# A reordered setup, the first tokens on SyncE's queue, and fill products in the projection's last step

## The reference, cut to what matters

```python
xn = layernorm(x)
# mixer
proj = xn @ in_proj_w + in_proj_b; v = proj[..., :d]
for i in range(2):
    ctrl = proj[..., (i + 1) * d:(i + 2) * d]
    h = implicit_filter(...)        # sin/cos of time -> gelu -> gelu -> linear, times exp(-|decay| t L)
    v = fft_conv(v, h)              # causal convolution over 2048
    xc = depthwise_conv3(ctrl) + conv_b
    v = v * xc * sigmoid(xc @ gate_w + gate_b)
attn = v @ out_proj_w + out_proj_b
# feed-forward: tern(w) = clip(round(w / scale), -1, 1), scale = mean |w| by row
r = relu(xn @ (tern(w_fc) * s).T + gate * (xn @ v.T @ fast_b.T @ u.T))
out = x + attn + (r * r) @ (tern(w_proj) * s).T
```

## Time and profile before

| | us |
|---|---|
| median of three runs | 929.61 (923.80, 929.61, 930.54) |
| profiled execution | 922.28 |
| its span, first to last instruction | 920.4 |
| setup, to the projection's first instruction | 0 to 67.6 |
| projection, to the last engine's block end | 67.6 to 367.2 |
| mixing and the output | 367.2 to 920.4 |

### The profile page before, as it was taken

How to read it: one execution, slowest core, us unless ns; L and a number is a source line. 1 busy time by engine, 2 the same in 40 slices (tenths; PEclk the granted TensorE clock), 3 DMA queues, 4 the chain that set the end, 5 groups by cost and what they waited for, 6 DMA issues and landing times.

```text
span 920.4 us, 25865 instructions
## 1 busy us (share of the span) xinstructions
PE 838.2 (91%) x9894; PEld 699.6 (76%) x9895; DVE 632.2 (69%) x1041; ACT 467.5 (51%) x678; POOL 242.6 (26%) x259
## 2 busy tenths in 40 slices
PE   3837999999999994899999999999999999999995
PEld 1325888888888883678888888788877888788995
DVE  6963799899899885455556555665655556666884
ACT  6422777777777874344444344444434444443221
POOL 1023564664664610201111121210112011210111
PEclk9977999999999998999999999999999999999998
DMA  5363223324324217776787878867787867962893
GB/s 176 116 210 131 100 92 136 138 91 147 127 91 159 93 70 205 188 166 138 167 191 158 174 150 188 188 156 175 140 193 170 184 127 165 202 112 69 232 333 124
DMA packets 84390, 142.02 MB, mean 154 GB/s; under 512 B 12837, under 2 KB 62390, under 8 KB 83318
## 3 DMA queue, kind: packets, MB, share of 16 engines
q1 hardware_dynamic: 73734, 102.79, 47.3%
q0 software_dynamic: 10320, 37.49, 12.7%
q10 hardware_dynamic: 288, 1.11, 0.4%
HBM read 97.39 MB, written 43.97 MB: 154 GB/s over the span
## 4 chain that ended last, share of the span: by engine, by line
PE 43%; DMA 8%; DVE 5%; issue 2%; ACT 1%; SPq 1%; POOL 0%; DVEq 0%; ACTq 0%; POOLq 0%
PE py L1262 12%; PE pp L1243 11%; PE pf L1215 10%; DMA lead<-filters 7%; PE pf L1221 2%; PE py L1299 2%; PE py L1230 2%; DVE r_lo L1060 1%; PE pp L417 1%; PE pp L419 1%; PE pp L418 1%; DVE r L1055 1%; DVE pp L1045 1%; DMA srow<-scales 1%; DVE xb L1050 1%
## 5 line engine op out<-in xcount | busy, mean ns | idle before, releaser
L1262 PEld LDWEIGHTS py<-vwin,lead 64*64 64x64 f32 x5120 | 133.4, 133 | 33.1 <-issue 33.1
L1262 PE MATMUL py<-vwin,lead 64*64 64x128 f32 (+4 forms) x5120 | 147.2, 265 | 8.1 <-DMA lead<-filters 7.4
L1161 ACT ACTIVATE r_hi<-r 128x512 fp32r<-128x512 f32 x128 | 80.9, 632 | 142.9 <-DVE r L1055 142.9
L1060 DVE TENSOR_TENSOR r_lo<-r,r_hi 128x512 fp32r<-128x512 f32 x128 | 103.3, 807 | 67.1 <-ACT r_hi L1161 67.0
L1156 ACT ACTIVATE r<-pf,fscale 128x512 f32<-128x512 f32 x128 | 88.0, 687 | 117.1 <-PE pf L1221 116.9
L1243 PE MATMUL pp<-wproj,r_hi 128*128 128x256 f32 x512 | 134.7, 296 | 8.3 <-DVE r_lo L1060 3.1
L1215 PE MATMUL pf<-tokens,split_a 128*128 (+1 forms) x512 | 139.5, 394 | 0.5 <-issue 0.5
L1243 PE MATMUL pp<-wproj,r_lo 128*128 128x256 f32 x512 | 126.8, 281 | 0.0
L458 POOL TENSOR_SCALAR lead<-lead,norms 128x256 f32<-128x256 f32 x64 | 114.0, 1792 | 3.4 <-POOL norms L452 3.4
L1243 PEld LDWEIGHTS pp<-wproj,r_hi 128*128 128x128 f32 x512 | 96.2, 188 | 21.3 <-issue 6.3
L618 DVE SCALAR_TENSOR_TENSOR xc<-ctrl,taps,xc 128x512 f32<-128x512 f32 x128 | 97.2, 779 | 18.8 <-ACT xc L690 18.1
(11 more groups left out here) (175 smaller groups left out, 1535.2 us busy)
## 6 DMA issues: line engine op xcount, KB each, us to landing
lead<-filters SPq DMA_DIRECT2D x128, 320.0 KB, 6.2
xnT_hbm<-split_b SPq DMA_DIRECT2D x32, 512.0 KB, 3.2
tokens<-xnT_hbm POOLq DMA_DIRECT2D x32, 512.0 KB, 7.4
lead<-in_attn_x SPq DMA_DIRECT2D x16, 512.0 KB, 3.9
gc_hbm<-xc SPq DMA_DIRECT2D x16, 512.0 KB, 2.6
GC<-gc_hbm SPq DMA_DIRECT2D x32, 256.0 KB, 7.1
out<-GC POOLq DMA_DIRECT2D x16, 512.0 KB, 5.8
GC<-in_attn_x POOLq DMA_DIRECT2D x9, 512.0 KB, 11.1
```

Source lines behind the costliest of these rows:

```text
L1060: dve.tensor_tensor(r_lo[j][:, :], r[j][:, :], r_hi[j][:, :].bitcast(F32), ALU.subtract).then_inc(r_split, 1)
L1161: act.activation(r_hi[j][:, :], r[j][:, :], ACT.Copy).then_inc(r_hi_done, 1)
L1262: last = pe.matmul(py[g % 2][q * BW:(q + 1) * BW, side, l, :, A:NB], tile[rows, q * PAIR + l, j * BW:(j + 1) * BW], vwin[g % 2][rows, q, l ...
```

## The change

Setup: frequency loads become two, small loads are reordered, and both natural weights and the rank operands are loaded from ScalarE's queue. `w1s` and `enc` cover 128 partitions, POOL clears the rest. Angles, layer 1 and layer 2 are handed over in halves and quarters of columns. Four products of ones and zeros are put on TensorE around the first small product. The four windows come together behind both Gelus. Statistics come before the filter tiles; the down matrix becomes ternary after them. The long peak reductions become ScalarE's sums of magnitudes. The low parts of the weights are made on POOL. SyncE's block end waits for four small stores, and the nine large ones are waited for by VectorE ahead of its first write of V in the projection. Projection: in the last step TensorE computes seven products into a free bank before the gates; the first tokens are loaded from SyncE's queue, with a semaphore of their own that mixing waits on.

```diff
-            sp.wait_ge(stored, 16 * 13)
+            sp.wait_ge(small_stored, 16 * 4)
...
+            pool.iota(prow[:, :], [[0, 1]], base=0, channel_multiplier=1).then_inc(row_ready, 1)
             pool.iota(jint, [[1, L]], base=0, channel_multiplier=0).then_inc(iota_ready, 1)
-            pool.iota(prow[:, :], [[0, 1]], base=0, channel_multiplier=1).then_inc(iota_ready, 1)
+            pool.wait_ge(iota_ready, 1)
+            pool.memset(enc[TIME_ROW:P, :], 0.0).then_inc(rest_ready, 1)
+            pool.wait_ge(rest_ready, 1)
...
             pool.wait_ge(eps_ready, 2)
             rstd(pool, 0, True)
             normalise(pool, 0, 0)
+            pool.wait_ge(hi_ready, 1)
+            pool.tensor_tensor(Win[1][:, :, :], win_f[:, :, :], Win[0][:, :, :].bitcast(F32), ALU.subtract)
+            pool.wait_ge(hi_ready, 2)
+            pool.tensor_tensor(Wgate[1][:, :, :], gw_f[:, :, :], Wgate[0][:, :, :].bitcast(F32), ALU.subtract)
...
-            link(dve.tensor_scalar(rnd, turns, ROUND, None, ALU.add))
-            link(dve.tensor_scalar(rnd, rnd, ROUND, None, ALU.subtract))
-            dve.tensor_tensor(turns, turns, rnd, ALU.subtract).then_inc(angle_ready, 1)
+            for h in range(2):
+                cols = slice(h * L // 2, (h + 1) * L // 2)
+                link(dve.tensor_scalar(rnd[:, cols], turns[:, cols], ROUND, None, ALU.add))
+                dve.scalar_tensor_tensor(out=turns[:, cols], in0=rnd[:, cols], scalar=ROUND, in1=turns[:, cols],
+                                         op0=ALU.subtract, op1=ALU.subtract).then_inc(angle_ready, 1)
...
+                dve.tensor_reduce(peaks[:, 0, w:w + 1], part, AX.X, ALU.max, apply_absolute_value=True).then_inc(peak_ready, 1)
+
+            dve.wait_ge(fc_in, 16)
+            thresholds(fc_nat, fsc, fth, HT, D)
+            ternary(fc_nat, fc_tern, fth, HT)
+            statistics(dve, 0, 0, True)
             filter_tile(0)
             filter_tile(1)
...
-            dve.wait_ge(hi_ready, 2)
-            dve.tensor_tensor(Win[1][:, :, :], win_f[:, :, :], Win[0][:, :, :].bitcast(F32), ALU.subtract)
-            dve.tensor_tensor(Wgate[1][:, :, :], gw_f[:, :, :], Wgate[0][:, :, :].bitcast(F32), ALU.subtract)
+            dve.wait_ge(rank_in, 16 * RANK_LOADS)
...
             filter_tile(2)
+            filter_tile(3)
+            dve.wait_ge(down_in, 16)
+            thresholds(pr_nat, psc, pth, KT, HID)
...
-            filter_tile(3)
...
-            statistics(dve, 0, 0, True)
...
+            ternary(pr_nat, pr_tern, pth, KT)
+
+            dve.wait_ge(srow_mm, 1)
+            dve.tensor_copy(srow[:, :], ps[:, 6, 0:D]).then_inc(srow_ready, 1)
...
         @block.scalar
         def _(act):
...
+            act.dma_start(fc_nat, w_fc.rearrange("(m p) d -> p m d", p=P)).then_inc(fc_in, 16)
+            act.dma_start(vs[:, :], v).then_inc(rank_in, 16)
+            act.dma_start(fbT[:, :], fast_b.rearrange("i j -> j i")).then_inc(rank_in, 16)
+            act.dma_start(gcol[:, :], bass.AP(gate.tensor, 0, [[0, P], [1, 1]])).then_inc(rank_in, 16)
+            act.dma_start(pr_nat, w_proj.rearrange("(k p) h -> p k h", p=P)).then_inc(down_in, 16)
+            act.dma_start(us[:, :, :], u.rearrange("(m p) r -> p m r", p=P)).then_inc(rank_in, 16)
+            act.wait_ge(warm_ready, 1)
+            act.activation(table[:, :], ones[:, 0:1], ACT.Sin)
+            act.wait_ge(t_ready, 1)
+            act.wait_ge(rest_ready, 1)
+            act.activation(enc[TIME_ROW:TIME_ROW + 1, :], t[TIME_ROW:TIME_ROW + 1, :], ACT.Copy).then_inc(t_row_ready, 1)
+            for h in range(2):
+                cols = slice(h * L // 2, (h + 1) * L // 2)
+                act.wait_ge(angle_ready, h + 1)
+                act.activation(enc[0:TIME_ROW, cols], enc[0:TIME_ROW, cols], ACT.Sin, scale=-TWO_PI).then_inc(enc_ready, 1)
...
+            for j in range(4):
+                act.wait_ge(l1_mm, j + 1)
+                act.activation(h1[:, j * 512:j * 512 + 512], ps[:, j, :], ACT.Gelu, bias=b1s[:, :]).then_inc(h1_ready, 1)
+            for j in range(4):
+                act.wait_ge(l2_mm, j + 1)
+                act.activation(h2[:, j * 512:j * 512 + 512], ps[:, j, :], ACT.Gelu, bias=b2s[:, :]).then_inc(h2_ready, 1)
+
+            act.wait_ge(ndec_ready, 1)
+            for w in range(4):
...
             act.wait_ge(proj_in, 16 * PROJ_LOADS)
             act.activation(Win[0][:, :, :], win_f[:, :, :], ACT.Copy).then_inc(hi_ready, 1)
-            act.wait_ge(l2_mm, 1)
-            act.activation(h2, lower, ACT.Gelu, bias=b2s[:, :]).then_inc(h2_ready, 1)
+            act.activation(Wgate[0][:, :, :], gw_f[:, :, :], ACT.Copy).then_inc(hi_ready, 1)
...
+            def far_sum(w):
+                part = hT[:, w, 0:L - FAR_FROM] if w < KT else hT[:, w, FAR_FROM:L]
+                act.wait_ge(h_ready, w + 1)
+                act.activation(junk[:, w, 0:L - FAR_FROM], part, ACT.Abs, accum_out=peaks[:, 1, w:w + 1]).then_inc(peak_ready, 1)
+
+            far_sum(0)
+            far_sum(1)
+            act.wait_ge(ternT_mm, 1)
+            act.activation(tern, upper, ACT.Copy).then_inc(ternT_ready, 1)
+            far_sum(2)
+            far_sum(3)
             act.wait_ge(uT_mm, 1)
             act.activation(ranks, upper[0:HALF, 0:HID], ACT.Copy).then_inc(ranks_ready, 1)
-            act.activation(Wgate[0][:, :, :], gw_f[:, :, :], ACT.Copy).then_inc(hi_ready, 1)
-            window(2)
-            window(3)
-            act.wait_ge(ternT_mm, 1)
-            act.activation(tern, upper, ACT.Copy).then_inc(ternT_ready, 1)
...
         @block.tensor
         def _(pe):
+            pe.wait_ge(warm_ready, 2)
+            for _ in range(2):
+                pe.matmul(ps[:, 7, :], ones[:, :], warm, start=True, stop=True)
             pe.wait_ge(rank_in, 16 * RANK_LOADS)
-            pe.wait_ge(ident_ready, 1)
             for k in range(KT):
                 last = pe.matmul(ps[:, 4, k * RANK:(k + 1) * RANK], vs[:, k * P:(k + 1) * P], fbT[:, :], start=True, stop=True)
             last.then_inc(m1_mm, 1)
-
+            for _ in range(2):
+                pe.matmul(ps[:, 7, :], ones[:, :], warm, start=True, stop=True)
+
+            pe.wait_ge(layer1_in, 16 * LAYER1_LOADS)
+            pe.wait_ge(t_row_ready, 1)
+            for j in range(4):
+                pe.wait_ge(enc_ready, j // 2 + 1)
+                pe.matmul(ps[:, j, :], w1s[:, :], enc[:, j * 512:j * 512 + 512], start=True, stop=True).then_inc(l1_mm, 1)
             pe.wait_ge(filter_in, 16 * FILTER_LOADS)
...
+                pe.wait_ge(h1_ready, j + 1)
+                pe.matmul(ps[:, j, :], w2s[:, :], h1[:, j * 512:j * 512 + 512], start=True, stop=True).then_inc(l2_mm, 1)
+            pe.wait_ge(ustack_ready, 1)
             for w in range(4):
                 if w >= 2:
                     pe.wait_ge(h_ready, w - 1)
                 o, c = w // KT, w % KT
                 for j in range(4):
+                    if w == 0:
+                        pe.wait_ge(h2_ready, j + 1)
...
+                    sp.wait_ge(gate_mm, 4 * NCH + KT)
+                    load_ahead[1](sp)
...
-            pool.wait_ge(gate_mm, 4 * NCH + KT)
-            pool.wait_ge(xn_saved[0], 16 * NCH)
-            pool.wait_ge(xn_saved[1], 16 * NCH)
-            load_ahead[1](pool)
...
+                    if s0 == 0:
+                        dve.wait_ge(stored, 16 * STORES)
...
+                if s0 == NCH:
+                    pe.wait_ge(xn_split, NCH)
+                    pe.wait_ge(gcT_mm, NCH)
+                    for _ in range(7):
+                        pe.matmul(pT[:, 0, :], ident[:, :], xnT[:, 0, :], start=True, stop=True)
...
-            pool.wait_ge(xn_loaded, 32)
+            pool.wait_ge(first_in, 32)
             load_xn(1, 1)
...
-                wait_alone(pe, xn_loaded, it * 32 + 32, pe_passed)
+                if first:
+                    pe.wait_ge(first_in, 32)
+                else:
+                    wait_alone(pe, xn_loaded, it * 32, pe_passed)
```

More of the change, by code:

```diff
@@ L39 @@
 ITERS = NCH // ORDERS
+STORES = 9
 ROUND = 12582912.0
@@ L48, with setup_stage @@
 HALF = PARTS * RANK
-def setup_stage(nc, hbm, ident, bv_row, flag, V, GC1, Wv, Win, Wgate, eps, half, load_first, norm, tern, ranks, fscale):
+def setup_stage(nc, hbm, ident, bv_row, flag, V, GC1, Wv, Win, Wgate, eps, half, load_x, load_taps, norm, tern, ranks, fscale, stored):
     (in_w, in_b, out_b, freqs, w1, b1, w2, b2, w3, b3, decay, gate_w, fast_b, w_fc, w_proj, u, v, gate,
@@ L94, in setup_stage @@
         ones = sb("ones", [P, P])
+        table = sb("sin_table", [P, 1])
+        junk = Gf[:, L:5 * L].rearrange("p (w j) -> p w j", w=4)
         win_f = sb("win_f", [P, KT, ORDERS * D])
@@ L159, in _ @@
                 load(w2s[rows, rows], w2[o], filter_in)
-                load(w3s[rows, o, :], w3[o], filter_in)
-            load(fc_nat, w_fc.rearrange("(m p) d -> p m d", p=P), tern_in)
-            load(pr_nat, w_proj.rearrange("(k p) h -> p k h", p=P), tern_in)
```

(33 more changed lines are left out.)

149 lines of the change are left out of this document (61 added, 88 removed).

## The result

| | median, us | runs | ratio to before [95% interval] |
|---|---|---|---|
| before, same session | 927.83 | 4 | |
| after | 917.94 (916.84 to 919.84) | 4 | 0.9881 [0.9849, 0.9913] |
| after, measured again | 914.01 | 4 | 0.9892 [0.9833, 0.9952] |

The change makes the kernel 1.1% to 1.2% faster, 10 to 11 us. The forecast was 912, from a gain of 17.5; the profiled execution after took 918.8 (span 917.1).

A forecast was written before the change was run, and what follows sets the result against it. Mixing is TensorE-bound and untouched, so the prediction looked to the setup's handover, projection's last step and start of mixing: 13.5 + 4.0 = 17.5 us off the median 929.6 gives 912, range 902 to 921.

The forecast's parts named there:

- second term: Projection's last step, block-end drain and start of mixing: 4.0 us gained together, bounds -1.9 to -5.5.
- -13.5: Setup: its handover to the projection comes at 54.1 us instead of 67.6; bounds -18 to -7.
- the port: Setup: POOL's new subtractions beside VectorE's filter tiles; POOL gives way, VectorE doesn't, so tiles stay at 2.35 us.
- the fill: Setup: fill products cost 3.4 us before layer 1, then two layer-1 products and layer 2 run at 2.4 GHz.
- the rival with 4.8 us for it: Setup: VectorE's tiles wait behind two POOL subtractions of 2.4 us; 917 us, chance 0.08.
- no store is late for V: Projection: large stores land at about 55 us, with 16 us of cover before the first V store.
- -4.0 for the last step, drain and start of mixing: Second block end: gates, drain and start of mixing gain 4.0 us together, not 1.9 + 3.0 + more.
- the drain's 3.0: Projection's block end: with token loads on SyncE, engines no longer wait for POOL's drain, gaining 3.0 us.
- the store, issued at 361.7 and landing 2.7 to 4.6 later: Start of mixing: last gated control's store lands at 364.4 to 366.3, taken as 365.6; TensorE starts 3.8 us earlier.
- the third rival: Second block end: gain lost to the store queued behind the tokens; 13.5 + 0 to 1.9, 915 us, chance 0.12.
- the gate products: Projection's last step: seven fill products bring the gates to 2.4 GHz, ending the second half's products 1.9 us earlier.
- the fourth rival: Mixing: more waiting for filter loads, now 7.4 us in seven waits; 930 to 940 us, chance 0.04.

The follow-up runs named there:

- no_fill4: The changed kernel without the four fill products in the setup: 915.56 us, 0.9883 of before.
- seam_only: The kernel before plus only the seven fill products and the first token loads on SyncE's queue with their semaphore: 924.94 us, 1.0007 of before.
- after_again: The changed kernel, unaltered, measured once more: 914.01 us, 0.9892 of before.
- setup_only: The changed kernel without the seven fill products, first tokens loaded from POOL's queue as before: 915.26 us, 0.9902 of before.
- lean kernels: Three variants of the changed kernel, loads the first rank product doesn't need put off: 920.95 us plain (0.9956), and lean_pooltok and lean_no_fill7.
- no_fill7: The changed kernel without the seven fill products of the projection's last step: 914.11 us, 0.9882 of before.
- no_fills: The changed kernel without any of the eleven fill products, four in the setup and seven in the last step: 911.02 us, 0.9823 of before.
- lean_no_fill7: The changed kernel with loads put off until the first rank product and without the seven fill products: 916.95 us, 0.9889 of before.
- before_again: The kernel before, unaltered, measured once more: 924.80 us, 0.9981 of before.
- wproj_late: The changed kernel with the 1 MB load of wproj moved behind the first rank operands: 919.50 us, 0.9934 of before.
- lean_pooltok: The changed kernel with loads put off until the first rank product, but first tokens on POOL's queue as before: 917.83 us, 0.9926 of before.

## Why the prediction was right, and where it was not

**Right: the time and the sign.** 917.94 in the first session lies in 902 to 921, the gain being 0.6 of the forecast's 17.5. The setup is the whole of it. The range was wide enough to hold a second term of 0, so that the time fell inside says nothing for that term.

**Right: the setup, nearly instant by instant.** Forecast and measured: rank products 10.8 to 11.8 and 11.86 to 12.8; layer 1 from 15.2 to 20.3, measured 16.39 to 20.1; the last Gelu to 24.5, measured 24.4; the first filter tile at 27.7, measured 27.8; the last tile finished at 40.3, measured 40.2; the new handover 54.1, measured 54.55 (the steps as the prediction lists them add up to 54.2, with the join 54.4, and not to 54.1). So -13.5 was -13.1. Inside it two small steps missed and made up for each other: the rank load came 1.1 us later than forecast, and layer 1 behind it was faster, 3.7 us instead of 5.1, because most of the clock's rise lay before it (0.93 over 16.39 to 20.30). That VectorE's first pass took 2.5 us instead of 1.3 (see the port below) and the frequency load came late cost nothing: TensorE was waiting for the rank load and then filling.

**Wrong within it: that the fill buys anything.** The prediction took the four products as a cost with a raised clock in return. no_fill4 shows that cost and return cancel.

**Right in its result, wrong in its reason: the port.** VectorE's filter tiles beside POOL's subtractions took what they took alone. The timeline of after, with POOL's operation and VectorE's tile of the same moment:

```profile
34.46 2.38 POOL L217 TENSOR_TENSOR split_a<-win_f,split_a 128x1024 fp32r<-128x1024 f32 x1 [2.63 <-ACT split_a L357]
...
34.50 2.35 DVE L283 SCALAR_TENSOR_TENSOR V<-ps_setup,b3s,V 128x2048 f32<-128x2048 f32 x1
```

So the rival with 4.8 us for it falls. But "POOL gives way, VectorE doesn't" is not what the traces show. The filter tile reads one of its two inputs from PSUM (`ps_setup`). Where both inputs are in SBUF, as in the squares `r<-r` of mixing, and VectorE starts behind POOL, VectorE waits. In after its operation of 0.68 us (the median of L1090) took 2.86:

```profile
409.57 2.57 POOL L1019 TENSOR_TENSOR xb<-xb,bo_row 128x1024 f32<-128x1024 f32 x1 [4.98 <-DMA xb<-in_attn_x]
...
409.84 2.86 DVE L1090 TENSOR_TENSOR r<-r 128x512 f32<-128x512 f32 x1
```

It ends 0.56 us behind POOL's. The kernel before has such pairs too: L1055 there has a median of 683 ns and a longest of 2780. The rule of the Trainium skill ("SBUF — State Buffer", section "SBUF: two separate sides"), that whoever starts first has the pair of ports for the whole instruction and the other fully blocks, names VectorE operations with two SBUF inputs or in a two-port mode. These rows agree with it, and it doesn't cover the filter tile; the prediction left that condition out. The 1.2 us that VectorE's first pass took too long look like the same wait. The pass starts 0.39 us behind a POOL memset of 1.80 and ends 1.08 behind it, where the cast of the same whole numbers took 1.23 in the kernel before. But the two are different operations, and no run has the pass without the memset, so this is not shown:

```profile
3.04 1.80 POOL L205 MEMSET GC<- 64x2048 f32 x1
...
3.43 2.49 DVE L243 TENSOR_SCALAR GC<-GC 128x2048 f32<-128x2048 int32 x1
```

**Right: that no store is late for V.** No wait on `stored` shows in the projection.

**Wrong: -4.0 for the last step, drain and start of mixing; it measured about 0 (seam_only, 1.0007 [0.9979, 1.0035]).** Its parts were right up to the block end: the last store earlier by 1.8 (forecast 1.9), the drain's 3.0 gone. One reading ahead of it was off: of the two token loads in the earlier trace rows the second, issued at 360.4, is the one that took 6.6 us. It landed at 367.0, not 366.2, and the drain ends 0.1 us behind it, not 0.9. So the drain ended with the tokens.

The step that failed is the next one, "the store, issued at 361.7 and landing 2.7 to 4.6 later". The 4.6 came from a store whose own queue was all but empty: the last load ahead of it landed 1.1 us after its issue, and the tokens were on POOL's queue. Here 1 MB of tokens stood in front of it in the same queue, behind the weights and filter rows, and it took 6.2 to 9.3 us in after, after_again and seam_only; `vrank`, which the working did not price at all, took 5.8 to 7.2 instead of 1.9. In after `vrank` came last, in the other two the store. The order in the queue is not the whole of it: in setup_only, with the tokens on POOL's queue again, the store still took 6.6.

From the store before the last to the landing of the last store it took 20.7 us before and 21.3 again, and 20.5 after, 22.6 again, 23.5 in seam_only, whatever the drain did. In it pass two stores (1024 KB), filter rows (1280 KB), first-layer weights (1280 KB) and tokens (1024 KB), 4.7 million bytes together. The two stretches of after below move 5.6 million bytes in 20 us (8.00 x 208 and 12.00 x 325), mixing's own loads, wproj's 1 MB among them, included, with the DMA engines busy all along:

```profile
335.92:343.92 8.00, 7.47 (x23) 4.01 (x22) 7.48 (x14) 4.99 (x9) 0.00 (x0) 1.00 0.94 208
...
343.92:355.92 12.00, 4.44 (x23) 3.17 (x21) 4.86 (x10) 4.18 (x7) 2.41 (x4) 0.81 1.04 325
```

(columns as in the earlier trace rows; the share of the DMA engines is 0.94 and 1.04.) That the transfers set the seam is shown from both sides, in single profiles: taking the drain and the slow gates away leaves it as long (seam_only), and putting loads off shortens it by 1 to 4 us against after and after_again (the lean kernels). It was the third rival, "the second seam gives its gain back", which had a chance of 0.12 and a time of 915; its mechanism was the true one, and its time the nearer to the two medians after, 917.9 and 914.0.

**Right for the kernel before, half as much in the one after: the gate products.** The forecast gave the seven fill products 1.9 us. With the old setup they bring the last store forward by 1.8 (seam_only 14.25, before 16.05). Against no_fill7 they are worth 0.9: behind the new setup the clock rises after seven of the gates without them (in setup_only, no_fills and lean_no_fill7 after seven or eight too). In the kernel before (`353.80:359.00` at clock 0.50) it had not risen in twelve.

**What stays open.** setup_only's handover is 14 us earlier than before_again's, but the medians are 9.5 apart (915.26 and 924.73). Two things take part. The profiled execution flatters it, 911.4 against its median of 915.3; and the handover itself varies, as the mean of nine, 55.3, shows: with it the setup's gain is 12.5. Some 3 us are still not accounted for. The profiles point to mixing. From the first to the sixteenth rank product it took 442.5, 444.6 and 444.8 us in the three profiles with the old setup, mean 444.0. In the eight with the new setup that are not lean the mean is 447.1: six took 444.4 to 446.1, and two, after and wproj_late, 452.9 and 452.2. The lean kernels took 451.3 to 457.1. Whether the new setup makes the long ones more frequent is not shown by two among eight. A good part of their excess is TensorE's wait for filter rows, the fourth rival's place: 11.5 and 11.3 us in the two, 5.9 to 9.4 in the nine others, 7.4 of them before. Two of these waits in after, of 2.18 and 2.37 us, were each followed by a stretch at the lower clock, in which 80 products took 3.45 and 3.74 us instead of 2.28. The rest is open, and no experiment here touched what makes it vary. The wait row of after, and the first of the two places in its timeline:

```profile
PE py L1300 <- DMA lead<-filters: 11.5, 9, 2.4
...
671.40 3.45 PE L1300 MATMUL py<-vwin,lead 64*64 64x128 f32 x80 [2.18 <-DMA lead<-filters]
```

## What to carry to other kernels

Taking away the wait that ends a stage gains only what the next wait behind it leaves over. Before a drain or a slow product is priced, lay the landings of the next stage's first loads along time, with what stands ahead of each in its queue, and take the later of the two. Chain shortening inside a stage (whole-tile passes cut into quarters, work moved to the idle engine) gave what the rows said. Products put in only to raise the clock should be measured against leaving them out; here taking them out never cost time.

## What the runs showed of the hardware

- The end-of-block drain of POOL stood for 7.05 us in the earlier trace rows and 9.42 us in setup_only with two token loads issued just ahead of it from POOL, and 7.65 and 7.62 us in before_again and lean_pooltok; in all four it ended 0.1 to 0.2 us after the second load had landed. Where SyncE issued them it was over 36 us before the block end.
- A 64 KB load (`vrank`) took 1.7 to 1.9 us where it was issued behind POOL's drain, 2.6 and 4.5 in two lean kernels, and 5.8 to 8.1 beside other loads of 0.5 to 1 MB; the last 64 KB behind 2 MB in one queue took 7.3 to 10.2 us in profiles with the new setup.
- In the last step TensorE had idled 6.9 us before the gates, and stood at 1.2 GHz for 12 products in both profiles of the kernel before and for 7 or 8 in four others (setup_only, no_fill7, no_fills, lean_no_fill7), the gates being the same.
- Within mixing, with TensorE at work for 95 to 97% of the time, the granted clock fell for a short stretch in some executions (twice in after and before_again, once in after_again, not in before). Each time TensorE had stood idle for 2.1 to 2.4 us just before (in after 2.18 and 2.37, waiting for filter rows). Over 458 us of it the mean is 1.00 in before and after_again, and 0.99 in after and before_again.
- A VectorE operation with both inputs in SBUF that started 0.27 us behind a POOL operation of 2.57 us took 2.86 us instead of 0.68 (after, 409.84); one with an input in PSUM, started 0.04 us behind POOL's, took its 2.35.
